# A two-layer graph network: dense adjacency products replaced by neighbour lists and gathered rows

## What is computed

```python
h = jnp.maximum(_layernorm(x, axis=-1), 0.0)
Wh = h @ W                                            # layer 0: attention over neighbours
e = jax.nn.leaky_relu(Wh @ a[:F_out] + (Wh @ a[F_out:]).T, 0.2)
att = jax.nn.softmax(jnp.where(adj > 0, e, NEG_INF), axis=1)
h_prime = att @ Wh
x = x + GRU(h_prime, h)                               # gates from w_ih, w_hh, b_ih, b_hh
h = jnp.maximum(_layernorm(x, axis=-1), 0.0)
x = x + adj @ (h @ W1.T + b1)                         # layer 1
```

## Time and profile before

| | |
|---|---|
| median of three runs | 1555.61 us |
| lowest and highest | 1553.42 and 1555.70 us |
| span of the profiled execution (first to last instruction) | 1552.9 us |
| instructions in the profile | 35381 |
| PE, DVE, ACT, POOL busy | 96%, 89%, 88%, 9% of the span |
| HBM read and written | 418.32 MB and 83.92 MB |

### The profile page before, as it was taken

One profiled execution on the slowest core, in us unless ns is written; L12 is line 12 of the kernel. 1 busy time (PEld: TensorE's weight loads), 2 busy tenths in 40 slices (PEclk: granted clock), 3 DMA queues, 4 the chain that ended last, 5 costly groups with the idle time before them and its releaser, 6 DMA issues.

```text
span 1552.9 us, 35381 instructions
## 1 busy us (share of the span) xinstructions
PE 1485.6 (96%) x13262; PEld 1304.4 (84%) x13262; DVE 1386.0 (89%) x2256; ACT 1369.6 (88%) x1972; POOL 136.2 (9%) x98
## 2 busy tenths in 40 slices
PE   5477999999999999999999999999999999999998
PEld 5356888888888888888888888888888888888887
DVE  8997999999999999999999999997579877766684
ACT  5779999999999999999999999996185998777785
POOL 5000011001100010001000100010000000000000
PEclk9778999999999999999999999999999999999999
DMA  8858999999999999999999999996386999888860
GB/s 314 298 204 332 365 350 360 352 366 353 355 357 370 352 349 353 374 351 357 359 365 345 362 362 355 349 360 265 122 354 238 408 361 352 308 304 310 321 228 16
DMA packets 96380, 502.93 MB, mean 324 GB/s; under 512 B 9599, under 2 KB 38985, under 8 KB 75337
## 3 DMA queue, kind: packets, MB, share of 16 engines
q1 hardware_dynamic: 78328, 444.54, 76.1%
q10 hardware_dynamic: 18000, 57.74, 9.8%
HBM read 418.32 MB, written 83.92 MB: 323 GB/s over the span
## 4 chain that ended last, share of the span: by engine, by line
PE 92%; DVE 5%; ACT 1%; issue 1%; DMA 0%; POOL 0%; DVEq 0%; ACTq 0%
PE ACC L1014 57%; PE ACC L1104 29%; PE GP L1040 2%; PE GP L1043 2%; PE GQ L1061 1%; ACT M L506 1%; DVE M L659 1%; DVE JK L642 1%; DVE TB L733 1%; DVE AE L728 1%; DVE JK L728 1%; PE TG L1027 0%; PE TG L1050 0%; DVE JK L646 0%; DVE M L751 0%
## 5 line engine op out<-in xcount | busy, mean ns | idle before, releaser
L1014 PE MATMUL ACC<-TB,M 128*128 128x258 f16 x8192 | 927.2, 275 | 41.8 <-DVE M L751 30.7
L1014 PEld LDWEIGHTS ACC<-TB,M 128*128 128x128 fp8e4 x8192 | 804.5, 98 | 150.7 <-issue 43.2
L506 ACT ACTIVATE M<-SB,dsteep 128x256 fp8e4<-128x256 f32 x1273 | 526.2, 538 | 0.0
L516 ACT ACTIVATE JK<-X 128x3328 uint8<-128x3328 uint32 x124 | 373.2, 3010 | 0.0
L692 DVE TENSOR_SCALAR Y<-X 128x4096 fp8e4<-128x4096 f32 x128 | 291.9, 2280 | 5.9 <-DMA X<-in_adjb_dram 5.5
L605 ACT ACTIVATE TB<-TB 128x8192 uint8<-128x8192 fp8e4 x32 | 225.0, 7030 | 76.5 <-DVE TB L890 71.7
L1104 PE MATMUL ACC<-WG,X 128*128 128x256 f16 x2048 | 225.5, 273 | 0.0
L1104 PE MATMUL ACC<-WG,TB 128*128 128x256 f16 x2048 | 225.4, 273 | 0.0
L1104 PEld LDWEIGHTS ACC<-WG,X 128*128 128x128 fp8e4 x2048 | 200.4, 98 | 23.2
L1104 PEld LDWEIGHTS ACC<-WG,TB 128*128 128x128 fp8e4 x2048 | 200.4, 98 | 23.1
L743 DVE TENSOR_SCALAR M<-SB,nd 128x256 fp8e4<-128x256 f32 x775 | 213.7, 345 | 0.0
...
## 6 DMA issues: line engine op xcount, KB each, us to landing
X<-in_adjb_dram SPq DMA_DIRECT2D x128, 2048.0 KB, 9.8
mask_bytes<-Y SPq DMA_DIRECT2D x128, 512.0 KB, 5.1
...
X<-mask_bytes SPq DMA_DIRECT2D x16, 2048.0 KB, 9.5
TB<-mask_bytes SPq DMA_DIRECT2D x16, 2048.0 KB, 9.1
M<-in_adjb_dram ACTq DMA_DIRECT2D x4, 2048.0 KB, 11.9
...
```

The costliest lines, as they stand in the source:

```text
L506: ins = nc.scalar.activation(rows(mask1(c), jj), SB[u][:, :], ACT.Sigmoid, scale=STEEP, bias=dsteep[:, j:j + 1], saturate=False)
L516: nc.scalar.activation(junk[:, 0:SEEN], X[c % 2][:, 0:SEEN].bitcast(u32), ACT.Sign, accum_out=nz[:, bass.ds(k, 1), at:at + 1].rearrange("p ...
L1014: ins = nc.tensor.matmul(A[t][m][:, 0:2 * TW], rows((mask1, mask2)[m](c), jj)[:, t * P:(t + 1) * P], TB[:, c * JC + jj, m, 0:2 * TW], star ...
```

## The change

`binary_adjacency` becomes `edge_lists`. The adjacency is now read in its own layout, rows on the partitions, each tile of 128 rows as two halves of 2 MB into four buffers `X`. There are 64 tiles, two to a slot, 32 slots and 6 more in which the pipeline empties. For each tile:

- **Codes.** TensorE adds 16 planes of 512 columns, each times a power of two, into one PSUM bank (`codes`, 16 products of 512 columns and two more): the number at a column says which planes have a one there. DVE first takes the diagonal out (`diagonal`).
- **Lists.** DVE takes the 16 largest codes of a row (`top`: `max`, `match_replace`, `max`), takes them apart (`decode`, 20 steps on 32 numbers) and gets up to 16 column indices for each row. A prefix sum on TensorE and the steps `compare`, `expand` and `select` pack the lists of a tile into 5 columns of 128 edges (640 edges at most, `CAP`).
- **Layer 0.** GpSimd gathers the projected rows of these edges from memory, ten indirect transfers of 128 rows for two tiles (`gather`). DVE makes the scores and one-hot matrices with the weights (`scores`, `onehot`), and TensorE sums rows into nodes (`aggregate`). The gates and the next norm stay much as they were, one to four slots later.
- **Counts.** ACT counts nonzero words (`nonzeros`) and DVE counts words equal to one (`ones_count`, with an accumulator output), both over all of every tile while it is in its buffer. With `NOW = 1` the list `late` is empty, so nothing is read a second time.
- **Layer 1.** After the stream GpSimd gathers rows of `layer_1_rows`, five indirect transfers for a tile, 320 in all; DVE makes plain one-hots, TensorE sums, DVE adds x.

The dense products, the byte store and its reload, the masks and their comparisons go. The core of the diff:

```diff
-                nc.vector.tensor_scalar(Y[c % 2][:, :].bitcast(f8), X[c % 2][:, :], 1.0, MARK, ALU.is_equal, ALU.mult,
-                                        saturate=False).then_inc(c_y, 1)
...
+                def ones_count(n, t):
+                    for d in range(2):
+                        h = 2 * t + d
+                        dve.wait_ge(x_in[h % 4], (h // 4 + 1) * 16)
+                        wait(dve, d_on, 2 * n + d)
+                        nc.vector.tensor_scalar(Q8[:, :], X[h % 4][:, :], 1.0, 0.0, ALU.is_equal, ALU.add,
+                                                accum_out=ON[:, h:h + 1]).then_inc(d_on, 1)
...
+                def top(t):
+                    u, kf = t % 2, KF[t // 2 % 2][:, t % 2, :]
+                    dve.wait_ge(c_v, t + 1)
+                    nc.vector.max(kf[:, 0:8], V[u]).then_inc(d_top, 1)
+                    dve.wait_ge(d_top, 3 * t + 1)
+                    nc.vector.match_replace(KR[u][:, :], kf[:, 0:8], V[u], -2.0 * TOP).then_inc(d_top, 1)
+                    dve.wait_ge(d_top, 3 * t + 2)
+                    nc.vector.max(kf[:, 8:16], KR[u][:, :]).then_inc(d_top, 1)
...
+                    dve.wait_ge(a_w, q + 1)
+                    for e in range(2 * KT5):
+                        c = 2 * KT5 * q + e
+                        ins = nc.vector.tensor_scalar(SW[q % 2][:, e, :], IO128, IE[:, c:c + 1], WE[q % 2][:, e:e + 1],
+                                                      ALU.is_equal, ALU.mult)
+                    ins.then_inc(d_oh, 1)
...
+                def codes(t):
+                    u = t % 2
+                    wait(pe, d_top, 3 * (t - 2) + 2)
+                    for d in range(2):
+                        h = 2 * t + d
+                        pe.wait_ge(x_in[h % 4], (h // 4 + 1) * 16)
+                        for k in range(8):
+                            ins = nc.tensor.matmul(V[u], DW[:, 8 * d + k, :], Xh[h % 4][:, k * GROUPS:(k + 1) * GROUPS],
+                                                   start=(d == 0 and k == 0), stop=False, skip_group_check=True)
+                        ins.then_inc(c_half, 1)
...
+                def gather(q):
+                    pool.wait_ge(d_sel, 10 * q + 5)
+                    wait(pool, ag_pe, q - 2)
+                    for e in range(2 * KT5):
+                        nc.gpsimd.indirect_dma_start(
+                            GB[q % 3][:, e, :], None, tab_d,
+                            bass.IndirectOffsetOnAxis(ap=IDX[:, 2 * KT5 * q + e:2 * KT5 * q + e + 1], axis=0)).then_inc(
+                                g_e[q % 3], 16)
...
+                def x_load(h):
+                    t = h // 2
+                    if h >= 4:
+                        sp.wait_ge(c_half, h - 3)
+                        before = (h - 4) // 2
+                        sp.wait_ge(d_dx, 2 * (before + 1))
+                        n = checked(before)
+                        if n is not None:
+                            sp.wait_ge(a_nz, 2 * n + h % 2 + 1)
+                            sp.wait_ge(d_on, 2 * n + h % 2 + 1)
+                    sp.dma_start(X[h % 4][:, :], adj[t * P:(t + 1) * P, (h % 2) * HALF:(h % 2 + 1) * HALF]).then_inc(
+                        x_in[h % 4], 16)
...
+                for n in range(SLOTS_N):
+                    for h in (4 * n + 4, 4 * n + 5):
+                        if h < 2 * NT:
+                            x_load(h)
+                    if 0 <= n - 2 < NS:
+                        rows_load(n - 2)
+                    for h in (4 * n + 6, 4 * n + 7):
+                        if h < 2 * NT:
+                            x_load(h)
...
+                    wait(pool, l_pe, t - 5)
+                    for e in range(KT5):
+                        nc.gpsimd.indirect_dma_start(
+                            GR[t % 6][:, e, :], None, g_d,
+                            bass.IndirectOffsetOnAxis(ap=IDX[:, KT5 * t + e:KT5 * t + e + 1], axis=0)).then_inc(
+                                g_r[t % 6], 16)
```

1506 lines of the change are left out of this document (718 added, 788 removed).

## The result

The changed kernel takes **2243.0 us** (median; 2241.8 to 2246.8), the kernel before 1555.2: a ratio of 1.443, with a 95% interval of 1.441 to 1.445. The forecast was 1959 and a range of 1570 to 2130. The direction was right and the size was not: 284 us are missing, more than the range allowed. The profiled execution has a span of 2245.1 us. One execution of the kernel before, beside the fourth group of experiments, was a slow one (5556.5 us) and is left out of every comparison.

What follows compares the result with a forecast made beforehand. The prediction took dense TensorE products as the old bound and DVE as the new. First stage 66, slots 1480, latency 15, stores 5, gathers 381 and end 9 gave span 1956, plus 2.7 around it: 1959 us, range 1570 to 2130.

Steps and rivals of the forecast that it cites:

- VectorE's work, 41.0 us a slot: Stream: DVE's priced steps for two tiles sum to 41.0 us, making DVE the new bound; four counts take 18.4.
- The wait on TensorE, 3.7 us (bounds 0.7 and 6.2): Head of a slot: DVE waits 3.7 us for codes queued behind the aggregation, so a slot is 44.7 us.
- Waits on top: Part on stream waits beyond DVE's work: 3.7 us for TensorE's queue, and SyncE's loop making 16 slots 47.8 us.
- The loop through SyncE: Odd tile's loads stand behind `rows_load`, which waits for an update: 16 slots of 47.8 us instead of 44.7.
- The first slots and the drain, 15 + 5: Stream's ends: last six slots make up the first slots' missing work, adding 15 us latency; last stores add 5.
- The first stage, 66 (bounds 50 and 78): Before the stream: adjacency loads queued ahead of column stores delay the columns; the first `top` comes at 66 us.
- Layer 1, 381 + 9: After the stream: 320 unhidden gathers at 1.19 us take 381 us; last tile, output and verdict take 9.
- The double rate: Rival on DVE's count of ones: four counts cost 9.8 us, a slot 36.1 or 39.2, time 1684; chance 0.23.
- The lock of GpSimd by VectorE: Rival: GpSimd is locked out by DVE; layer 1's gathers wait to 2.15 us each, time 2266; chance 0.05.
- the change pays: Rival: double-rate count and gathers under 0.79 us together; at 0.60 the time is 1495 us; chance 0.13.
- What would show it: Signs: count pass 4.4 or 2.3 us, slots 45 and 48, DVE over 85%, TensorE under 60%, layer 1 380 us.
- the three ways in which the prediction called itself wrong: Count of ones runs double, gathers are far from 1.19 us, or top-16 steps are not one number a cycle.

Runs made afterwards that it cites:

- the fourth group of experiments: Changed kernel with GpSimd two tiles ahead, not five: 2182 us; one product a layer-1 tile: 2187; reordered split count, ScalarE's sums last in the slot: 1645; also later odd loads: 1641.
- with codes ahead: Changed kernel with odd codes first in the slot, next even codes ahead of the aggregation on TensorE, and SyncE's odd loads ahead of row loads: 1874 us.
- the kernel with both orders mended: Changed kernel with odd codes directly behind even codes on TensorE and odd tile's loads ahead of row loads on SyncE: 1943 us.
- the repeated run: The changed kernel once more, without an edit: 2237 us.
- the first group: Changed kernel with odd codes behind even codes: 1987 us; odd loads ahead of row loads: 2151; both: 1943; count of ones on 8 columns: 1720.
- the added products: Changed kernel with eight more bfloat16 products of 512 columns for each tile of layer 1, into an unused bank: 2258 us.
- the runs meant to tell it: Changed kernel with GpSimd two tiles ahead of TensorE in layer 1, not five: 2182 us; with one product a layer-1 tile, not five: 2187 us.
- The fifth group: Split-count kernel with `scores` and one-hots behind `select`, ScalarE's `edge_weights` and sums behind `row_steps`: 1556 us; also with the odd tile's first loads later: 1555 us.

## Why the prediction was wrong, point by point

- **VectorE's work, 41.0 us a slot: right within 4%.** It is 39.5 in the changed kernel; with codes ahead a slot is 40.2 us, 1.0 of it a wait. The single-rate count at 4.43 (4.41), six passes of the top 16 and the short dependent steps came out nearly as priced. That the accumulator costs the double rate was argued then and is shown now (2.30 against 4.41).
- **The wait on TensorE, 3.7 us (bounds 0.7 and 6.2): the step that failed.** The part "Waits on top" followed TensorE's queue only behind the aggregation, at the head of a slot. There it was right in kind, 4.8 us in the kernel with both orders mended. But a slot asks for codes twice. I did not walk the queue for the odd tile, where `prefix`, `attended` and `normed` stand ahead of the codes, and `normed` needs what VectorE does last. That is 6.4 to 6.5 us in each slot, hidden by nothing, where the prediction had 0. Both waits on TensorE together are 10.0 us a slot in the first half and 6.5 in the second. With that order mended, and nothing else, slots are 44.4 and 46.1 to 48.0, where the forecast had 44.7 and 47.8. That they meet so well is in part luck: in the first half 1.5 us too much for the work stand against 1.6 too little for the waits at the head.
- **The loop through SyncE: right in its place, but made longer by the same step.** In the second half it was to add 3.1 us. The loop runs from the odd tile's count over `update`, the row loads and the loads to the diagonal, and the wait for the odd codes lies inside it, so the slot there is 53.6 and not 47.8. From the first row load (1003.88) to the diagonal (1018.90) are 15.0 us, forecast as 14.8, though with 2 us to land where its own row (9.8 less 5.9) gives 3.9.
- **The first slots and the drain, 15 + 5: right as a sum.** The drain took 65 us, and the first slots were 38 us short, so with 32 full slots 21 us are left. The drain's longest waits are for gathers that nothing covers any more, 10 of 1.25 us and the landing: 7.6 and 10.9 us before `scores` at 1723.8 and 1748.7.
- **The first stage, 66 (bounds 50 and 78): 78.3**, and 73.2 in the repeated run. VectorE waited until 70.5 for ScalarE's features, and then 5.2 us for the first codes.
- **Layer 1, 381 + 9: the gather was nearly right (1.25 against 1.19), the rest was not seen.** Clean, it takes 414 us. The other 55 us come in eight stretches like this one (TensorE, VectorE in order of time):

```profile
1793.81 0.29 DVE L923 TENSOR_TENSOR H<-ACC,WG 128x128 f32<-128x128 f32 x1 [5.21 <-PE ACC L1142]
...
1797.59 2.47 PE L1142 MATMUL ACC<-H 128*128 128x128 f32 x10 [3.81 <-DMA H<-layer_rows,IDX]
...
1816.24 0.29 DVE L923 TENSOR_TENSOR H<-ACC,WG 128x128 f32<-128x128 f32 x1 [21.16 <-issue]
...
1828.84 0.37 PE L1142 MATMUL ACC<-H 128*128 128x128 f32 x1 [1.74 <-issue]
...
1831.62 0.37 PE L1142 MATMUL ACC<-H 128*128 128x128 f32 x1 [2.42 <-issue]
...
1838.64 0.29 DVE L923 TENSOR_TENSOR H<-ACC,WG 128x128 f32<-128x128 f32 x1 [21.13 <-PE ACC L1142]
```

  `finish` of the third tile starts 16 us after that tile's ten passes, and at 1828 to 1832 a pass is recorded each 2.8 us. They came in the run of the result and with every kernel of three groups that issues five gathers a tile (GpSimd idle 151 to 159 us), and with none of the two others (104 to 105). TensorE's low clock is not enough to cause them: layer 1 is clean at 0.50 in the first group and has them at 0.69 with the added products. Nor is it the order of the stream, which differs between kernels of one group. With one gather a tile they are gone on a chip that has them, and with more products they come more often; whether the number of outstanding gathers or TensorE's queue is the cause stays open, since the runs meant to tell it fell on a clean chip.
- **The rivals.** The double rate did not come. The lock of GpSimd by VectorE is real, but in these runs only beside double-rate comparisons: no gather of the changed kernel takes over 1.23 us, and the lock appeared when the experiments brought the double rate back. Neither condition of "the change pays" was met, since the count took 4.41 us and a gather 1.25, not under 0.79. The fifth group came level with the kernel before (1556) by another way: the queues of four engines reordered, half of the tiles counted in layer 1 and the rest compared on VectorE and summed on ScalarE.
- **What would show it.** Right: 4.4 us, TensorE under 60% below full clock, 1.25 us from gather to gather, the gap before the even `max` (3.6 in the first half, but 0 in the second). Wrong: VectorE over 85% busy (73), slots of 45 and 48 (51 and 54), 3 us before the diagonal of the odd tile (7.6), a layer 1 of 380 us (469). None of the three ways in which the prediction called itself wrong came true: the step that failed was not among its doubts.

By terms, of the 289 us between the spans: 197 from the slots, 1 from the first slots and the drain, 12 from the first stage, 24 from layer 1's gathers and end, 55 from the stretches. The odd codes alone are over 200, and VectorE's lighter work gives some of it back. Without the stretches, of which the trace before shows nothing, the time would still lie outside the range, at some 2188.
